# Side pieces of a two-layer Flamingo block placed by a written plan instead of by weighted counts

## What is computed

```python
def cope(query, attn_logits, pos_emb):
    gates = sigmoid(attn_logits)
    pos = minimum(flip(cumsum(flip(gates))), npos_max - 1)
    logits_int = einsum('bhqd,dn->bhqn', query, pos_emb)
    # interpolate logits_int between ceil(pos) and floor(pos)
x = x + tanh(g_xattn[0]) * cope_attention(layernorm(x), ctx)
x = x + tanh(g_ffn[0])   * (top2_of_8_experts(layernorm(x)) + shared_expert(layernorm(x)))
x = x + tanh(g_xattn[1]) * cross_attention(layernorm(x), ctx)
x = x + tanh(g_ffn[1])   * gated_attention(layernorm(x))
```

## Time and profile before

| | us |
|---|---|
| median of 3 runs (5251.74 to 5252.87) | 5252.0 |
| profiled execution | 5251.9 |
| its span, first to last instruction | 5250.2 |
| VectorE busy | 3946.1 (75%) |
| TensorE busy | 3337.5 (64%) |
| ScalarE busy | 2428.4 (46%) |
| GpSimd busy | 1397.6 (27%) |
| mean granted TensorE clock | 0.715 of 2.4 GHz |

### The profile page before, as it was taken

One profiled execution on the slowest core, in us unless ns is written; L12 is line 12 of the kernel. 1 busy time (PEld: TensorE's weight loads), 2 busy tenths in 40 slices (PEclk: granted clock), 3 DMA queues, 4 the chain that ended last, 5 costly groups with the idle time before them and its releaser, 6 DMA issues.

```text
span 5250.2 us, 64557 instructions
## 1 busy us (share of the span) xinstructions
PE 3337.5 (64%) x21126; PEld 2217.6 (42%) x21126; DVE 3946.1 (75%) x8619; ACT 2428.4 (46%) x5505; POOL 1397.6 (27%) x1125
## 2 busy tenths in 40 slices
PE   3347575665757667575665757667575665757676
PEld 2225253443625335353443625335363443525353
DVE  3698687786977778696786968778696776868753
ACT  2454444444444444544444444444544454444432
POOL 0342223223232222223223222222323222222300
PEclk7558586776858668686776858668686776858687
DMA  4000000000000000000000000000000000000000
GB/s 125 8 5 1 1 11 1 11 1 11 1 1 11 1 11 1 1 11 1 11 1 11 1 1 11 1 11 1 3 9 1 11 1 10 1 1 7 1 7 3
DMA packets 42691, 40.93 MB, mean 8 GB/s; under 512 B 6468, under 2 KB 42342, under 8 KB 42360
## 3 DMA queue, kind: packets, MB, share of 16 engines
q1 hardware_dynamic: 42360, 36.85, 2.3%
HBM read 32.64 MB, written 4.19 MB: 7 GB/s over the span
## 4 chain that ended last, share of the span: by engine, by line
DVE 44%; PE 26%; issue 12%; ACT 12%; POOL 3%; DVEq 0%; POOLq 0%; ACTq 0%; DMA 0%; SPq 0%
DVE banks L713 7%; DVE row_negmax L1252 5%; DVE masks L704 4%; PE banks L287 4%; DVE u L941 4%; DVE steps L729 4%; PE banks L356 4%; PE banks L265 3%; PE banks L789 3%; DVE c L675 3%; PE banks L320 3%; DVE eg_eth L959 2%; PE banks L278 2%; DVE o L968 2%; DVE steps L735 2%
## 5 line engine op out<-in xcount | busy, mean ns | idle before, releaser
L618 POOL TENSOR_TENSOR steps<-slope,rises 128x512 f32<-128x512 f32 x256 | 302.6, 1182 | 2951.3 <-DVE masks L704 2357.2
L713 DVE COPY_PREDICATED banks<-masks,banks 128x448 f32<-128x448 int16 (+5 forms) x1536 | 1028.1, 669 | 28.3
L789 PE MATMUL banks<-xn,w 128*128 128x256 f16 x6912 | 852.5, 285 | 111.2 <-ACT h L861 111.2
L789 PEld LDWEIGHTS banks<-xn,w 128*128 128x128 f16 x6912 | 693.7, 102 | 273.8 <-ACT h L861 139.1
L704 DVE TENSOR_SCALAR masks<-shift 128x512 int16<-128x512 int16 x1536 | 334.7, 288 | 438.5 <-ACT shift L546 434.8
L1252 DVE TENSOR_REDUCE row_negmax<-banks 128x4 f32<-128x1024 f32 x256 | 306.1, 1215 | 159.7 <-PE banks L341 159.7
L632 POOL TENSOR_TENSOR partial<-partial,core_scores 128x512 f32<-128x512 f32 x256 | 357.2, 1395 | 0.1
L675 DVE TENSOR_TENSOR_SCAN c<-gate,cap 128x514 f32<-128x514 f32 x256 | 341.6, 1335 | 1.0 <-ACT gate L530 1.0
L443 PE MATMUL banks<-table,core_queries 64*128 64x256 f16 x512 | 124.6, 333 | 339.5 <-ACT slope L593 339.5
L861 ACT ACTIVATE h<-banks,b 128x256 f32<-128x256 f32 x576 | 238.6, 465 | 216.3 <-PE banks L789 216.1
L622 POOL TENSOR_TENSOR partial<-slope,neg_rest 128x512 f32<-128x512 f32 x256 | 330.4, 1291 | 2.1 <-DVE negmax L735 2.1
(11 more groups left out here) (262 smaller groups left out, 7462.7 us busy)
## 6 DMA issues: line engine op xcount, KB each, us to landing
stage<-in_L_ffn_w SPq DMA_DIRECT2D x16, 512.0 KB, 5.5
ahead<-in_ctx SPq DMA_DIRECT2D x32, 128.0 KB, 2.2
ahead<-in_x SPq DMA_DIRECT2D x32, 128.0 KB, 2.3
u<-in_ctx SPq DMA_DIRECT2D x32, 128.0 KB
x<-in_x SPq DMA_DIRECT2D x32, 128.0 KB
out<-x SPq DMA_DIRECT2D x32, 128.0 KB, 1.8
stage<-in_L_ffn_w SPq DMA_DIRECT2D x8, 256.0 KB, 6.1
stage<-in_L_ffn_sw SPq DMA_DIRECT2D x2, 512.0 KB, 4.4
```

What stands on the lines that cost most here:

```text
L618: nc.gpsimd.tensor_tensor(k.steps[:, g % 2], k.slope[:], k.rises[:, g % 2], ALU.mult)\
L713: move = nc.vector.copy_predicated(tab[:, :, 0:S - b], k.masks[:, n, :, 0:S - b], tab[:, :, b:S])
L789: last = nc.tensor.matmul(k.bank[bank][:, f * S:(f + 1) * S], w[:, e, a, c, par, f * P:(f + 1) * P], k.x_parts[:, b, c, :], start=(n == 0) ...
```

## The change

The weights and the rule that shares pieces out are replaced by a table, `PLAN`. For each of a batch's 16 slots, and a 17th entry that goes with slot 0 of the next batch, it gives two strings with one letter per piece. The digits say where VectorE does the piece: 0 to 4 after copy n, 5 after scan L675, and a new place 6 after the slot's reductions. The letters put it on TensorE and ScalarE into the first group, the middle group, or a new last group behind the table product (TensorE) and behind `whole_part` (ScalarE). The slots now hold 3, 3, 3, 3, 3, 4, 4, 4, 18, 12, 8, 3, 3, 18, 14, 6 and 1 pieces: 0-2, 3-5, 6-8, 9-11, 12-14, 15-18, 19-22, 23-26, 27-44, 45-56, 57-64, 65-67, 68-70, 71-88, 89-102, 103-108, 109. The side starts one slot later (`LAG` 4), there are two more slots in all, and the ahead pieces are spread otherwise: a batch starts at s % 16 = 8 with two pieces, and two are done at s % 16 = 12. No instruction of the computation is added or removed. Line numbers after the change are 7 to 13 higher. The two loops on GpSimd, the first groups and the callers change only in form:

```diff
--- before.py
+++ after.py
@@ -72,8 +72,6 @@
-PHASES = [0.5] * (H + 1) + [1.4] * (H + 1)
-PIECE_TIMES = [4] * (4 + 2 * NE) + [2] * 2 + [6] * 4 + PHASES + [5] * 3 + [3.5] * 7 + PHASES + [4] * 4
@@ -103,24 +101,33 @@
-LAG = 3
-PIECES = [0] * H
-for at in range(len(PIECE_TIMES)):
-    PIECES[int((sum(PIECE_TIMES[:at]) + PIECE_TIMES[at] / 2) * H / sum(PIECE_TIMES))] += 1
-FIRST = [(2 * n + 1) // 3 for n in PIECES]
-AHEAD = [1, 1, 0, 1, 1, 2] + [1] * (H - 6)
+LAG = 4
+MAXIMA = ("0" + 4 * "2" + 4 * "3" + 4 * "4" + 4 * "6" + "6", 5 * "F" + 12 * "M" + "L")
+PLAN = [("136", "FMM"), ("245", "FFM"), ("135", "FFM"), ("135", "FFM"), ("135", "FFM"), ("1245", "FFFM"),
+        ("1245", "FFML"), ("1346", "FFML"), MAXIMA, (12 * "5", 5 * "F" + 7 * "L"), ("00000346", "FFFFFMMM"),
+        ("346", "FMM"), ("046", "FMM"), MAXIMA, (14 * "5", 6 * "F" + 8 * "L"), ("000346", "FFFMML"), ("1", "F")]
+AHEAD = [1, 1, 1, 1, 1, 1, 0, 0, 2, 1, 1, 1, 2, 1, 1, 1]
 G = B * H
-SLOTS = G + H + LAG
+SLOTS = G + H + LAG + 1
+
+
+def side_plan(s):
+
+    b, q = divmod(s - H - LAG, H)
+    rest = PLAN[H] if q == 0 and 1 <= b <= B else ("", "")
+    new = PLAN[q] if 0 <= b < B else ("", "")
+    return rest[0] + new[0], rest[1] + new[1]
 
 
 def side_pieces(s):
 
-    return (PIECES[(s - LAG) % H], FIRST[(s - LAG) % H]) if s >= H + LAG else (0, 0)
+    groups = side_plan(s)[1]
+    return groups.count("F"), groups.count("M"), groups.count("L")
 
 
 def ahead_pieces(s):
 
-    return AHEAD[s % H] if s >= 5 and s < G + 5 else 0
+    return AHEAD[s % H] if s >= 8 else 0
@@ -469,10 +476,12 @@
-        for _ in range(pieces - first):
+        for _ in range(middle):
             next(side)
         if s + 1 < G:
             table(s + 1)
+        for _ in range(final):
+            next(side)
         for _ in range(ahead_pieces(s)):
             next(ahead, None)
...
@@ -683,9 +694,9 @@
-    def some_pieces(pieces, n):
-
-        for _ in range((n + 1) * pieces // len(MOVES) - n * pieces // len(MOVES)):
+    def some_pieces(places, n):
+
+        for _ in range(places.count(str(n))):
             next(side)
@@ -737,6 +748,7 @@
             dve.wait_ge(sem["core_z_ready"], NT * (g + 1))
+        some_pieces(places, len(MOVES))
         for _ in range(ahead_pieces(s)):
             next(ahead, None)
```

More of the change, by code:

```diff
@@ L456, in core_tensor @@
     for s in range(SLOTS):
-        pieces, first = side_pieces(s)
+        first, middle, final = side_pieces(s)
         if 6 <= s < G + 3 and s % 4 == 2:
@@ L636, in core_pool @@
             pool.wait_ge(sem["core_rest"], s + 1)
-        for _ in range(side_pieces(s)[0]):
+        for _ in range(sum(side_pieces(s))):
             next(side)
@@ L697, in core_vector @@
     for s in range(SLOTS):
-        pieces, _ = side_pieces(s)
-        if s >= H + LAG and s % H == LAG:
+        places = side_plan(s)[0]
+        if H + LAG <= s < SLOTS - 1 and s % H == LAG:
             head_sums(s // H - 1)
@@ L715, in core_vector @@
                     moved = step(move, wait=False)
-                    some_pieces(pieces, n)
+                    some_pieces(places, n)
                 else:
@@ L720, in core_vector @@
             for n in range(len(MOVES) - 1):
[L721 removed]
+                some_pieces(places, n)
         if s + 1 < G:
             scan(s + 1)
[L724 removed]
+        some_pieces(places, len(MOVES) - 1)
         g = s - 1
```

2 lines of the change are left out of this document (removed).

## The result

The changed kernel takes 5322.7 us (median of 4 runs, 5302.15 to 5343.94) against 5251.87 us for the kernel before, run beside it: a ratio of 1.0135, 95% interval 1.0084 to 1.0186. It is slower by 71 us, and the forecast of 5214 us and its range (5130 to 5290) were wrong. Two of its runs lie near 5304 us and two near 5342, hence the wide interval, and the trace is of one of the former (5305.73 us).

A forecast was written before the change was run, and what follows sets the result against it. No engine bound throughout; VectorE's waits were priced. Waits 58.5 to 56.4 us and 0.8 less elsewhere shorten a batch by 2.9; 14.7 batches give 43 less, run start and tail 5 more: 5251.9 becomes 5214 us, range 5130 to 5290.

The forecast's parts named there:

- Shift: VectorE's masks waiting for ScalarE's shift behind exponentials: 8.4 us per batch left of 30.1, so 21.7 go.
- Heads: VectorE's wait at the heads for the last exponentials and products, both attentions: 27.0 us per batch instead of 2.3.
- `add_to_x`: VectorE's wait for the y projections, now hidden by scans and reductions: about 1.2 of 6.0 us per batch stays.
- Gated query: VectorE's wait for the gated attention's query, covered by scan and reductions: 1.1 of 3.6 us per batch stays.
- Gate logits: VectorE's wait for the gate's logits, 1.3 us per batch before, covered at place 6: 0.
- Norms: VectorE's waits at the norms: 3.3 of 3.8 us per batch stay.
- Scores: VectorE's wait for scores after the query stacks, both attentions: 7.0 us per batch instead of 10.1.
- The ends: Start and tail of the run, outside the steady overlapped batches: 5 us more in all.
- The tiny instructions: VectorE's L984, 1.19 us while GpSimd ran: routing moves to place 4, one norm likewise, 2 us less per batch.
- What is added: VectorE's new waits for the core's ahead key and query parts: 2.5 and 5.9 us per batch, bounds 0 to 14 together.
- A: Slower: ahead parts hold VectorE's queue and the masks, 6 us more per batch, 5302 us; chance 0.24, shared with smaller slowdowns.
- B: Much faster: TensorE at 2.4 GHz in the last group's heads, 8 us less per batch, 5096 us, half 5155; chance 0.18.

The follow-up runs named there:

- e8: Changed plan with the ahead pieces of before (5119.1 us), plus the last groups' seven and eight exponentials as middle groups, ahead of slope and shift: 5110.2 us.
- e12: Changed kernel with only VectorE's own part of ahead pieces 3 and 4 moved behind the second copy of the next slot: 5273.9 us.
- e3: Changed kernel with ahead piece 15, the core's values copied for the products, one slot earlier (slot 4 instead of 5): 5323.0 us.
- e1: Changed kernel with its plan of pieces, but the ahead pieces where the kernel before had them: 5119.1 us, ratio 0.9751 to the kernel before.
- e5: Changed kernel with only ahead pieces 0 to 4 early as before the change, pieces 5 to 15 left late: 5181.1 us, ratio 0.9869 to the kernel before.

## Why the prediction was wrong

**Right, by its own steps** (forecast, then the batch after). Shift 8.4 and 8.5. Heads 27.0 and 26.1, one of them 14.6 us. `add_to_x` 1.2 and under 0.3, and no load arrived late. Gated query 1.1 and 1.2. Gate logits and the gated attention's scaled query 0, and neither is in the list of after. Norms 3.3 and 2.7. Scores 7.0 and 6.1. The most surprising sentence, that the heads take back nearly all that the shift gives, held, and e8 supports its reason. The ends, forecast at +5, seem to hold as well, but by luck. Against before, the scan of head 16 is 1.3 us later, the batch from head 16 to head 32 18.2 shorter, the last 15 slots 2.1 and what is behind the last scan 17.6 longer, +2.8 together. That is what 13 batches leave over. Beside the 14.7 batches of the forecast the ends make -4: 54 us in all, less 14.7 x 3.9.

**The tiny instructions.** The routing's instruction of the earlier trace rows fell from 1.19 to 0.23 us as forecast, but VectorE's busy time rose by 0.3 us. A gain of 2 us was expected there, and 1.2 more for the copies, which measured 65.1 us (64.9 before). The slowed instruction is another one: the gate's L1325, of 2 elements, takes 1.19 us where it took 0.16, and the scan at 2148.13 takes 2.22, where the longest scans before took 1.84.

**What failed: "What is added".** The step priced the two ahead parts at 2.5 and 5.9 us, and they measured 4.2 and 8.1 as waits. It took 1.9 us for either projection, half the slow price, and they took 2.63 and 3.78. The bounds (0 to 14) held the waits' sum. The choice between the bounds was wrong, and it alone is 4 us of a batch. The deeper fault is that I priced the ahead row by VectorE's waits there and nothing else. Measured as the whole row, late ahead pieces cost 13.3 us per batch against 8.4. In the query part the price lay mostly outside VectorE's queue: e12 moves VectorE's part back and leaves 3.6 of 4.9 us. By the rows it is ScalarE's queue that passes it on. ScalarE waits 3.12 us for the projection and does two copies ahead of the core's work and of the query stacks, whose chain sets the exponentials' start. I had used these times only to find when VectorE could go on. The rest of the 13.3, 2.9 us outside stretches 11 and 12, I had left at nothing; 1.5 of it is in stretch 9 and 1.1 in stretch 6, where the late values stand (e3).

**The sum.** Without its ahead waits my batch would have been 310.7 - 8.4 = 302.3 us. e1, which has next to none of them (0.3 us in the batch read), measures 304.7. So the plan was forecast 2.4 us too short and the ahead row 4.9 too cheap, 7.3 together (318.0 - 310.7). Half a us of this is that the forecast began from a batch of 313.55 and the mean is 314.1; from there the error is 6.8 us per batch, 100 in 14.7, and with the ends 9 us below the forecast it gives 5214 + 100 - 9 = 5305, the profiled run.

**The rivals.** A came: 5302 us by its price, 5305.7 in the profiled run. That these agree so well is partly luck. The two waits are 3.9 us above the forecast's and not 6, and the rest comes from terms that A didn't have. Its mechanism, that the ahead parts hold VectorE's queue, is the key part's; the query part's is, by the rows, ScalarE's queue. I gave it 0.24 although it needed only 3 us more than I assumed, in a step whose bounds were 14 us apart. B hardly came. The mean clocks of the two stretches with seven and eight heads in the batch read are 0.82 and 0.66. Before the change the exponentials were spread over two stretches in either attention, at 0.50 and 0.67 in the cross attention and 0.50 and 0.83 in the gated one. The heads came 0.9 us sooner than forecast. But B's mechanism is real, and the changed kernel's own trace shows it. These are two of its batches, stretch 3 (the gated attention), with the same instructions:

```profile
3833.75:3863.44 29.69, 20.54 (x146) 10.25 (x146) 10.42 (x24) 16.57 (x36) 5.48 (x5) 0.66 0.04 10
4151.31:4177.28 25.97, 15.86 (x146) 8.69 (x146) 10.41 (x24) 16.45 (x36) 5.48 (x5) 0.87 0.03 10
```

At a mean clock of 0.87 the stretch is 3.7 us shorter, near the 4 us per attention that B had priced, with ScalarE busy for as long. Ten of the 12 batches have 29.7 us at 0.66, and one each 28.9 at 0.70 and 26.0 at 0.87. What B had wrong is how often the fast clock comes. The Trainium skill, TensorE: Matmul & The Clock Gate, Part 1 (sustained activity releases the throttle) names activity as the cause. The rows show the levels and what they cost, but not why one batch of twelve got the higher one.

**What stays open.** Why the late last eleven pieces cost 62 us alone and nothing beside the late first five is not known; of e5's 4.9 us per batch over e1, 2.1 are in stretch 6 and 1.7 in stretch 14. Nor is it known where the missing 2.4 us of the plan are, of which the scores' wait in e1 (11.2 us in the batch read, with 7.0 forecast) is a part. Lengths of the exponentials' stretches move by 1 to 2 us per batch between the traces with the clock that was granted, so that differences of that size between two kernels' batches have no cause shown.

## What to carry to other kernels

A piece of work off the critical path is nearly free where the engine that would wait for it is itself behind, and is paid for where that engine is ahead (the query part: 1.6 us in one place, 4.9 in the other): before such a piece is moved, read the busy share of the stretch that it comes from and of the one that it goes to. Price a moved piece on every queue that it goes through, and most of all as a delay of what stands behind it on the engines ahead of the last one (here ScalarE's two copies), since a wait that is taken from the consumer comes back under another name. Of a change with two tables, run each alone: here one was worth 132 us and the other cost 204.
